# Three of the twelve groups of record scatters beside the slice attention's main loop go beside the stage of its output

## The reference

```
def _L0_ffn_ref(x, W_fx, b_fx, W_x, b_x, W_slice, b_slice, W_q, W_k, W_v, W_out, b_out, temperature):
    ...
    fx_mid = (x @ W_fx + b_fx).reshape(B, N, H, D).transpose(0, 2, 1, 3)
    x_mid = (x @ W_x + b_x).reshape(B, N, H, D).transpose(0, 2, 1, 3)
    slice_weights = jax.nn.softmax((x_mid @ W_slice + b_slice) / temp, axis=-1)
    slice_norm = slice_weights.sum(axis=2)
    slice_token = jnp.einsum('bhnc,bhng->bhgc', fx_mid, slice_weights)
    slice_token = slice_token / (slice_norm[..., None] + 1e-05)
    ...
    attn = jax.nn.softmax(jnp.einsum('bhgc,bhkc->bhgk', q, k) * SCALE, axis=-1)
    out_slice = jnp.einsum('bhgk,bhkc->bhgc', attn, v)
    out_x = jnp.einsum('bhgc,bhng->bhnc', out_slice, slice_weights)
    out_x = out_x.transpose(0, 2, 1, 3).reshape(B, N, INNER)
    return out_x @ W_out + b_out

def _L2_gnn_ref(h, edge_indices, edge_attr, W1, b1, W2, b2, W_ih, b_ih, W_hh, b_hh):
    row, col = (edge_indices[0], edge_indices[1])
    edge_in = jnp.concatenate([h[row], h[col], edge_attr], axis=-1)
    ...
```

## Time and profile before

| what | value |
|---|---|
| median of the runs | 6393.75 us (6391.69 to 6400.41) |
| profiled execution | span of 6396.8 us, 72731 instructions, mean granted TensorE clock 0.896 |
| TensorE busy | 4980.4 us (78%) |
| VectorE busy | 3277.9 us (51%) |
| ScalarE busy | 1623.8 us (25%) |
| GpSimd busy | 3406.6 us (53%) |
| all record scatters (L554) | 416 in three places of the program |
| slice attention's main loop, small stage, output stage | 1730.7 to 1883.0, 1883.7 to 1913.4, 1914.0 to 1976.9 us |

### The profile page before, as it was taken

One profiled execution on the slowest core, in us unless ns is written; L12 is line 12 of the kernel. 1 busy time (PEld: TensorE's weight loads), 2 busy tenths in 40 slices (PEclk: granted clock), 3 DMA queues, 4 the chain that ended last, 5 costly groups with the idle time before them and its releaser, 6 DMA issues. The chain is left out here.

```text
span 6396.8 us, 72731 instructions
## 1 busy us (share of the span) xinstructions
PE 4980.4 (78%) x20184; PEld 3081.3 (48%) x20185; DVE 3277.9 (51%) x7777; ACT 1623.8 (25%) x3879; POOL 3406.6 (53%) x3602
## 2 busy tenths in 40 slices
PE   7968877887676888788863997799988568888455
PEld 2233334333445333355652886688875333343244
DVE  8954444444456777776772112566656332444412
ACT  4920002000323888511111221233331111000111
POOL 3147774777151777777735655467730211777223
PEclk7979998999788999888876998899999779999777
DMA  5023342334111000233323774333330334333255
GB/s 198 5 77 104 103 100 74 104 103 102 29 34 25 2 2 2 58 97 97 97 46 120 226 218 150 95 114 115 114 73 2 114 102 135 103 104 103 38 177 175
DMA packets 405943, 597.93 MB, mean 93 GB/s; under 512 B 131551, under 2 KB 305952, under 8 KB 405472
## 3 DMA queue, kind: packets, MB, share of 16 engines
q0 software_dynamic: 144992, 337.62, 20.1%
q1 hardware_dynamic: 257392, 252.99, 12.9%
q10 hardware_dynamic: 3216, 3.28, 0.2%
HBM read 472.47 MB, written 121.17 MB: 93 GB/s over the span
## 5 line engine op out<-in xcount | busy, mean ns | idle before, releaser
L784 PE MATMUL ps<-wide 128*128 128x256 f32 x2640 | 915.5, 429 | 323.0 <-DMA wide<-table,src 188.6
L811 DVE TENSOR_TENSOR sums<-sums,ps 128x256 f32 x1320 | 555.2, 421 | 981.8 <-PE ps L784 979.0
L769 POOL DMA_INDIRECT wide<-table,src x880 | 852.6, 969 | 276.5 <-PE ps L784 203.2
L784 PEld LDWEIGHTS ps<-wide 128*128 128x128 f32 x2640 | 407.3, 190 | 844.3 <-DMA wide<-table,src 557.6
L781 PE MATMUL ps<-zerow,zerob 128*128 128x440 bf16 x2640 | 713.4, 352 | 28.2 <-DVE wide L126 28.2
L769 POOL DMA_INDIRECT wide<-table_rel,rel x440 | 428.7, 974 | 351.5 <-ACTq L95 217.8
L1737 POOL DMA_INDIRECT wide<-table_gat,src x440 | 477.0, 1084 | 148.1 <-issue 122.8
L2379 POOL DMA_INDIRECT work<-table,work x440 | 451.8, 1027 | 187.8 <-issue 107.2
L1625 POOL DMA_INDIRECT work<-table_max,src x440 | 452.4, 1028 | 134.3 <-issue 134.3
L1644 PE MATMUL ps<-wide,work 128*128 128x512 f32 x880 | 451.1, 594 | 0.0
L1606 ACT ACTIVATE wide<-ident,work 128x128 f32<-128x128 f32 x1320 | 416.2, 388 | 64.9 <-DMA work<-table_max,src 61.1
(11 more groups left out here) (474 smaller groups left out, 9031.7 us busy)
## 6 DMA issues: line engine op xcount, KB each, us to landing
wide<-in_L_ffn_W SPq DMA_DIRECT2D x64, 1024.0 KB, 6.0
wide<-in_L_ffn_expert_w SPq DMA_DIRECT2D x90, 256.0 KB, 3.2
table_rel<-wide SPq DMA_DIRECT2D x20, 1024.0 KB, 4.4
work<-rows_in SPq DMA_DIRECT2D x62, 256.0 KB, 5.7
rows_out<-work SPq DMA_DIRECT2D x62, 256.0 KB, 3.5
work<-rec SPq DMA_DIRECT2D x110, 136.0 KB, 2.2
rec<-work SPq DMA_DIRECT2D x27, 544.0 KB, 16.5
wide<-table,src POOLq DMA_INDIRECT x880, 2.8
```

The source lines that it names most:

```text
L769: nc.gpsimd.indirect_dma_start(rows[:, w % RT, :], None, table, bass.IndirectOffsetOnAxis(ap=index[:, w:w + 1], axis=0)).then_inc(gathered ...
L784: nc.tensor.matmul(m.PS[:, w % (2 * Q), 0:D], S[:, w % RT, :], rows[:, w % RT, :], start=True, stop=True).then_inc(summed, 1)
L811: v.tensor_tensor(at, at, m.PS[:, s, 0:D], ALU.add).then_inc(added, 1)
```

## The change

A new constant `BESIDE = 17` splits groups 8 to 19. Groups 8 to 16 stay beside the main loop; groups 17, 18 and 19 are loaded and sent by a new SyncE and a new GpSimd program in the output stage, with the same two buffers and five semaphores of that stage's own.

```
+BESIDE = 17
...
-            for n in range(EARLY - PLACED):
+            for n in range(BESIDE - PLACED):
                 if n >= 2:
                     sp.wait_ge(sent[n % 2], n // 2 * 16 * SG)
                 load_group(sp, a["edge_attr_64"], records, PLACED + n, n % 2, arrived)
             for u in range(2):
-                sp.wait_ge(sent[u], (EARLY - PLACED) // 2 * 16 * SG)
+                sp.wait_ge(sent[u], len(range(u, BESIDE - PLACED, 2)) * 16 * SG)
...
-            send_groups(nc, pool, m, records, range(PLACED, EARLY), arrived, sent, filled)
+            send_groups(nc, pool, m, records, range(PLACED, BESIDE), arrived, sent, filled)
...
     with Stage(nc) as st:
         names = ("staged", "turned", "copied", "made", "biased", "taken")
         staged, turned, copied, made, biased, taken = (st.sem(s) for s in names)
+        filled = st.sem("filled")
+        arrived, sent = st.sems("arrived", 2), st.sems("sent", 2)
+        records = view(xn, 5280, 2 * SG, EA + 4)
...
+        @block.sync
+        def _(sp):
+            for n in range(EARLY - BESIDE):
+                if n >= 2:
+                    sp.wait_ge(sent[n % 2], n // 2 * 16 * SG)
+                load_group(sp, a["edge_attr_64"], records, BESIDE + n, n % 2, arrived)
+            for u in range(2):
+                sp.wait_ge(sent[u], len(range(u, EARLY - BESIDE, 2)) * 16 * SG)
+
+        @block.gpsimd
+        def _(pool):
+            send_groups(nc, pool, m, records, range(BESIDE, EARLY), arrived, sent, filled)
```

## The result

The changed kernel takes 6372.45 us in the median of 6 runs (6357.72 to 6378.62), the kernel before beside it 6395.7 (6389.37 to 6404.34, 6 runs). The ratio is 0.9959, 95% interval 0.9948 to 0.997: 0.41% less, about 26 us. The two medians themselves differ by 23.3 us. The forecast was 6367.5, the range 6359 to 6378. The profiled execution has a span of 6366.6 us at a mean granted clock of 0.9.

What follows compares the result with a forecast made beforehand. Stages end in barriers, and GpSimd's drain was taken to bound the main loop's stage. Own span 6396.8 less 26.3, with 0 for the output stage, contact and clock, gave 6370.5, put against the median as 6367.5 us; range 6359 to 6378.

Steps and rivals of the forecast that it cites:

- The bound of the main stage: End of the main loop's stage: GpSimd's drain holds the barrier until 1883.0, 7.9 us behind the last scatter.
- 26.3 us less: Main loop's stage: with nine groups the barrier's end goes from GpSimd's drain at 1883.0 to VectorE's at 1856.7.
- The tail of nine groups: GpSimd's drain behind 72 main-loop scatters: 0, 7.9 or 13.1 us, in each case over before VectorE's drain.
- Slack of the output stage: Output stage: three moved groups with tail take 44.2 us, at worst 49.4, of 62.7, adding 0 to the path.
- The tail term: Output stage: 7.9 us of drain behind the 24 moved scatters, read from the main stage's tail with 96.
- The 1.0 us between groups: Output stage: time counted between groups of eight scatters at 1.27 us each, making 11.2 us a group.
- the five semaphores and the busy GpSimd: Barrier behind the output stage: cost taken as 0, bounded by the whole gap of 1.19 us once more.
- No contact with VectorE: Output stage: VectorE's 25 additions slowed by scatters would cost 1.7 us at 67 ns each; 0 was taken.
- The rival of the shared ports: Output stage: each of 24 scatters stops VectorE for 0.971 us, adding 23.3 us, giving 6390.8; chance 0.05.
- The clock: Small stage: TensorE expected at the low clock level again, as before; 0 taken, at most 3.4 us lost.
- The gain bound of 8.8: TensorE from 1885 to 1920: 19.60 us busy at clock 0.55 would take 10.8 at the high level.
- The slower rival: Output stage: stalls beside scatters keep TensorE's clock low, adding 49.4 us, giving 6416.9; chance 0.03.

Runs made afterwards that it cites:

- run 1: Changed kernel with ten groups (80 scatters) beside the main loop and two in the output stage: 6369.29 us, ratio 0.9964 to the kernel before.
- run 3: Changed kernel with all loads and scatters of groups 8 to 19 left out: 6361.93 us, ratio 0.9958 to the kernel before.
- run 5: Changed kernel with six groups beside the main loop, on one buffer in place of two, and six in the output stage: 6387.42 us, single execution.

## Why the prediction was right

The forecast was 6367.5 us in a range of 6359 to 6378. The median came at 6372.45, inside it, and 5.0 above the forecast; the kernel before, measured beside it, was itself 2.0 higher than its earlier median.

- **The bound of the main stage** (GpSimd's drain, 7.9 us behind the last scatter). Right, and shown: in the kernel before every other engine was done by 1876.4 and the barrier waited for the drain until 1883.0, in run 1 the drain alone ends the stage, and in run 3, without any scatters there, the stage takes 126.7 us, where the changed kernel has 126.9. On the slower chip, where the drain isn't the bound, the ratio is 0.9989, with an interval that reaches 1.
- **26.3 us less.** The barrier's end went from 1883.0 to 1857.6 with a stage that began 2.8 us later (1730.3 to 1733.1); the term itself is right. The measured ratio gives 26.2 in all and the medians 23.3. That the first fits so closely is partly luck: the compute of this stage alone differs by 2.5 us between executions of one kernel, and the output stage gave 1.1 that no term of the sum had.
- **The tail of nine groups** was bounded by 0, 7.9 and 13.1. It is 5.9 (1841.86 to 1847.8), and didn't enter the sum.
- **Slack of the output stage.** 4.0 us to the first scatter: 1892.38 less 1888.65 is 3.7. Counted from the stage's first load, the scatters end after 35.6 (36.3 predicted), the drain at 1926.5 after 37.9 (44.2 predicted with the tail of 96). The tail term was too long by 5.6, since a drain behind 24 scatters has 2.3. The 1.0 us between groups was too long too: its own rows give 1.95 from start to start where 1.27 is usual, so 0.7. Neither cost anything, as the slack was larger. For the five semaphores and the busy GpSimd 0 was taken, and the gap behind the stage is 1.14 for 1.19.
- **No contact with VectorE.** Run 3: 0.3 us at most in a stage. The rival of the shared ports is out for this kernel; its price of 23.3 us was a bound without support. Nor did VectorE's 25 copies hold up GpSimd: from the first moved scatter's start to the last one's end it is 31.85 us, under the 32.3 counted for them. On the slower chip this stays untested.
- **The clock.** The level in the small stage stayed low, as forecast (0.61 for 0.56 in the first profiled execution, and 30.4 us in both). What moved was elsewhere: 1.8 us of compute in the main stage and 1.1 in the output stage. The gain bound of 8.8 was fair: with TensorE kept busy 6.6 us are had.
- **The slower rival** (clock lost beside the scatters) didn't occur: 0.97 in the output stage with and without them.

## What to carry to other kernels

Where a stage ends in a barrier, read each engine's drain at it, and not only the last instruction or the engine to which the idle time is put down. GpSimd's drain ended 1.9 to 7.9 us behind its last scatter here, and up to 13.1 behind a last gather. Background work is free just up to the slack of the stage that hides it, so count the slack with the tail. And count it on the chip that will run the kernel: where the main stage took 181.5 us in place of 127, the same change gave 0.11% in place of 0.41%.

## What was not expected

**The drain's tail grows with the number of scatters.** Behind 16, 24, 40, 48, 56, 72, 80 and 96 scatters of these two stages it is 1.9, 2.3, 3.3, 4.0, 4.6, 5.9, 6.6 and 7.9 us, which is 0.08 us for each more from 40 on (7.9 less 3.3, by 56) and less below. Behind 48 it is the same whether GpSimd paused between groups or not (run 5). What it does in that time isn't shown. Nor does the line hold everywhere: in the kernel before it fits the 64 scatters of the stage that sorts the edges, with 5.3 us, but behind the 256 beside the paired experts it would give some 20, and there are 5.3 again (the last scatter ends at 3912.69, the drain at 3905.8 + 12.2 = 3918.0). The six loops of 440 gathers in that kernel have tails of 8.7 to 13.1, of which the prediction read one, so the count isn't all that sets the tail. No run here tells what does.

**Matmuls that nobody reads make a chain of short steps faster.** In the small stage 21.17 us of TensorE's 24 are busy, most of it for nothing, and the chain takes 6.2 us less on that chip and 5.2 on the one at 0.90. Its own matmuls run at the high level for all of it in the first case and for most of it in the second.
